# Routed experts moved into the block of the second graph layer, with gathers two blocks ahead

## The reference

```python
x = x + gnn(layernorm(x))      # two layers: aggregate over edges, add the residual product, relu
y = layernorm(x)
logits = softmax(relu(y @ router_w1 + b1) @ router_w2 + b2)
top_w, top_i = top_k(logits, 2); weights = softmax(top_w)
h1 = relu(y @ expert_w1[e] + b1[e]); h2 = relu(h1 @ expert_w2[e] + b2[e])
x = x + sum over the two chosen e of weight * (h2 @ expert_w3[e] + b3[e])
```

## Time and profile before

| | us |
|---|---|
| median of 3 runs (2244.78 to 2249.43) | 2246.9 |
| the profiled execution | 2250.68 |
| its span | 2249.0 |
| busy PE, DVE, ACT, POOL | 1913.3, 1201.6, 828.8, 334.9 |

### The profile page before, as it was taken

The page is one execution under the profiler, slowest core; times in us unless marked ns, Lnnn a source line. Parts: engine busy times, 40 slices in busy tenths (PEclk is TensorE's granted clock), DMA queues, the critical chain, the costliest instruction groups (busy, mean ns, idle before and its releaser), DMA issues. The chain is left out here.

```text
span 2249.0 us, 38317 instructions
## 1 busy us (share of the span) xinstructions
PE 1913.3 (85%) x12396; PEld 1155.2 (51%) x12396; DVE 1201.6 (53%) x2678; ACT 828.8 (37%) x1921; POOL 334.9 (15%) x350
## 2 busy tenths in 40 slices
PE   3458917999999999999979999999997199986765
PEld 3444504555555555555535555455554088865554
DVE  8995606666666666666514444444444244433333
ACT  3805715565656556565502222221222022221111
POOL 1006100000000000000001111211212023344444
PEclk9999968999999999999989999999998599999999
DMA  6002283333223332333375454554553588855552
GB/s 197 0 0 63 68 162 88 143 141 138 109 111 142 138 138 97 125 142 138 132 293 189 171 213 182 182 217 167 200 198 111 174 267 269 276 171 203 190 198 93
DMA packets 117038, 350.59 MB, mean 156 GB/s; under 512 B 18798, under 2 KB 79942, under 8 KB 110712
## 3 DMA queue, kind: packets, MB, share of 16 engines
q1 hardware_dynamic: 90140, 297.18, 37.6%
q0 software_dynamic: 16480, 40.14, 5.3%
q10 hardware_dynamic: 10364, 12.64, 1.7%
HBM read 209.41 MB, written 150.46 MB: 160 GB/s over the span
## 5 line engine op out<-in xcount | busy, mean ns | idle before, releaser
L1178 PE MATMUL bank<-parts,counts 128*128 128x512 f16 x2401 | 643.3, 378 | 0.0
L1178 PE MATMUL bank<-parts,counts_again 128*128 128x512 f16 x2401 | 540.2, 380 | 11.8 <-DMA counts_again<-counts_table 10.5
L1325 ACT ACTIVATE counts<-bank 128x392 f16<-128x392 f32 x800 | 395.1, 497 | 363.4 <-PE bank L1241 356.7
L1178 PEld LDWEIGHTS bank<-parts,counts_again 128*128 128x128 f16 x2401 | 235.5, 100 | 280.4 <-issue 14.1
L580 DVE TENSOR_TENSOR rows_lo<-pair_keys,iota_lo 128x2048 bf16<-128x2048 bf16 x200 | 245.0, 1225 | 239.2 <-PE bank L1241 239.2
L1241 PEld LDWEIGHTS bank<-rows_hi,rows_lo 128*128 128x128 bf16 x3200 | 227.6, 99 | 256.8 <-DVE rows_hi L580 65.3
L1241 PE MATMUL bank<-rows_hi,rows_lo 128*128 128x98 bf16 x3200 | 277.9, 210 | 64.0 <-DVE rows_hi L580 63.1
L454 POOL DMA_INDIRECT first_rows<-route_rows,route_spot_i x49 | 48.2, 984 | 1402.0 <-DVE tokens L445 1394.7
L1178 PEld LDWEIGHTS bank<-parts,counts 128*128 128x128 f16 x2401 | 192.5, 96 | 103.6 <-issue 1.1
L580 DVE TENSOR_TENSOR rows_hi<-pair_keys,iota_hi 128x1568 bf16<-128x1568 bf16 x200 | 193.8, 969 | 0.0
L1949 ACT ACTIVATE h_t<-bank,w 128x256 f32<-128x256 f32 x120 | 56.9, 474 | 295.1 <-PE bank L1898 295.1
(11 more groups left out here) (223 smaller groups left out, 1981.8 us busy)
## 6 DMA issues: line engine op xcount, KB each, us to landing
counts_table<-counts SPq DMA_DIRECT2D x25, 3136.0 KB, 9.2
counts_again<-counts_table SPq DMA_DIRECT2D x24, 3136.0 KB, 12.8
w<-expert_pack SPq DMA_DIRECT2D x60, 898.0 KB, 5.2
rows<-first_rows SPq DMA_DIRECT2D x30, 514.0 KB, 6.7
res_tile<-res_table SPq DMA_DIRECT2D x98, 128.0 KB, 2.2
rows<-second_rows SPq DMA_DIRECT2D x30, 258.0 KB, 5.0
res_table<-res_tile SPq DMA_DIRECT2D x49, 128.0 KB, 1.7
res_table<-res_next SPq DMA_DIRECT2D x49, 128.0 KB, 6.2
```

What stands on the lines that cost most here:

```text
L1178: mm = nc.tensor.matmul(acc[:, 0:2 * dim], lhs, rhs, start=s == 0, stop=s == tiles)
L1325: nc.scalar.activation(counts[:, b, :, :].rearrange("p s (o n) -> p o s n", o=2)[:, :, :, q * QUAD:(q + 1) * QUAD], bank[4 + q % 4][:, 0:Q ...
```

## The change

The experts no longer have a block of their own. Their instructions stand in `sum_and_route`, behind or between those of the last pairs, in a class `Work` whose methods are called from each engine's code.

- VectorE makes an early list (`early_list`) while pair 23 is summed, from the rows placed up to pair 21. It holds 17 blocks of first choices (`EARLY_BLOCKS`) which are certain to be full. The rest of the list is made later (`final_list`).
- Blocks 0 to 5 are loaded as soon as the scatters of pairs 0 to 21 have landed and SP is through with its own last pair; the weights once pair 23 is summed, since they now lie in the second buffer of `counts_again`.
- The last part of routing is split over the steps of the first blocks by functions `beside(b)`, which each engine calls in its step b. The zeros behind each expert's rows are written by POOL in steps 8 to 13.
- `index` and `gather` are two blocks ahead instead of one, and `index(b + 2)` stands ahead of `add_bias(b)`. `outs` has one bank per block and signals once per block, and waits for the result of two blocks ago instead of one.
- `turn` has one bank in place of two, and the router's four banks are now one. The marks for `count_before` are bf16.

```diff
@@ sum_and_route, SP
                     by_pairs(sp, pair)
+                    work.early_rows(sp)
+                    sp.wait_ge(update.sums_ready, 2 * LAST_PAIR)
+                    work.early_weights(sp)
+                    work.loads(sp)
@@ TensorE
+                    def beside(b):
+                        if b == 0:
+                            pe.wait_ge(update.sums_out, tiles)
+                        if b == 1:
+                            router.count_before(pe, LAST_PAIR - 1, 2)
+                        if b == 4:
+                            router.turn(pe, LAST_PAIR, 0, 1)
+                        if b == 5:
+                            router.hide(pe, LAST_PAIR, 1)
+                        if b == 6:
+                            router.logits(pe, LAST_PAIR, 1)
+                        if b == 8:
+                            router.count_before(pe, LAST_PAIR, 1)
+                    work.products(pe, beside)
@@ VectorE
+                    def beside(b):
+                        if b == 0:
+                            router.choices(dve, LAST_PAIR - 1, 2, False)
+                        if b == 1:
+                            router.gates(dve, LAST_PAIR - 1, 1, 2)
+                        if b == 2:
+                            router.place(dve, LAST_PAIR - 1, 1, 2, False)
+                            router.variance(dve, LAST_PAIR, 1)
+                        if b == 3:
+                            router.normal_rows(dve, LAST_PAIR, 0, 1)
+                        if b == 6:
+                            router.shift_logits(dve, LAST_PAIR, 1)
+                        if b == 7:
+                            router.choices(dve, LAST_PAIR, 1, True)
+                        if b == 8:
+                            router.gates(dve, LAST_PAIR, 0, 1)
+                            router.place(dve, LAST_PAIR, 0, 1, True)
+                            work.free_rows(dve)
+                        if b == 9:
+                            work.final_list(dve)
@@ class Work
+                def loads(self, sp):
+                    def after(first):
+                        def body(b, k):
+                            sp.wait_ge(result_ready, b + 1)
+                            self.load_weights(sp, b + WB, k)
+                            if first is not None:
+                                self.load_rows(sp, b + SB, k, first)
+                        return body
+                    for b in range(2 * SB):
+                        if b + SB == EARLY_BLOCKS:
+                            sp.wait_ge(list_ready, 2)
+                            sp.wait_ge(rest_cleared[0], 16 * experts)
+                            router.wait_scattered(sp, pairs)
+                        after(True)(b, b)
...
+                def add_outs(self, dve, b, k, c):
+                    dve.wait_ge(bias_added, b + 1)
+                    dve.wait_ge(outs_ready, b + 1)
...
+                    def steps(r, c, start=False, last=False):
+                        for k in range(SB):
+                            b = r * SB + k
+                            self.high(dve, b, k, 1, h2_bank, h2_t, h2_ready, h2_high_out)
+                            if not (last and k + 1 >= SB):
+                                self.high(dve, b + 1, (k + 1) % SB, 0, h1_bank, h1_t, h1_ready, h1_high_out)
+                            if isinstance(b, int) and b < 2 * SB:
+                                beside(b)
+                            if not (last and k + 2 >= SB):
+                                into = 1 if isinstance(r, int) and b + 2 >= NB else c
+                                self.index(dve, b + 2, (k + 2) % SB, r + (k + 2) // SB, into)
+                            if c:
+                                dve.wait_ge(first_back[k % 3], (r - NB // SB) * (32 * SB // 3) + 32 * (k // 3 + 1))
+                            self.add_bias(dve, b, k, c)
...
+                            self.add_outs(dve, b, k, c)
...
+                    for b in range(3 * SB):
+                        self.scatter(pool, b, b, first_out)
+                        beside(b)
+                        if b == 8:
+                            pool.wait_ge(free_ready, 1)
+                        if 8 <= b < 8 + len(clears) // 2:
+                            for c, e in clears[2 * (b - 8):2 * (b - 7)]:
+                                self.clear(pool, c, e)
...
+                    for b in range(NB, NB + 2):
+                        self.gather(pool, b, b)
+                    def second(b, k):
+                        self.gather(pool, b + 2, k + 2)
+                        self.scatter(pool, b, k, out)
```

More of the change, by code:

```diff
@@ L236, with __init__ @@
     STEPS = 36
-    def __init__(self, nc, sb, sem, shapes, tables, weights, consts, placed_to, tokens, banks):
+    def __init__(self, nc, sb, sem, shapes, tables, weights, consts, placed_to, tokens, turns):
         self.nc = nc
@@ L455, in scatter, with wait_scattered_to @@
                                         bounds_check=table.shape[0] - 1, oob_is_err=False).then_inc(self.scattered[b], 16)
+    def wait_scattered_to(self, eng, i):
+        for b in range(2):
+            eng.wait_ge(self.scattered[b], SCATTERS * 16 * ((i + 1) // 2))
     def wait_scattered(self, eng, pairs):
@@ L474, in gnn_moe_kernel @@
     K2 = dim // P
+    pairs = -(-tiles // 2)
     ROWS = 2 * P
@@ L480, in gnn_moe_kernel @@
     table_rows = experts * region + idle * ROWS
+    EARLY = pairs - 4
+    EARLY_BLOCKS = -(-((EARLY + 1) * 2 * P - experts * (ROWS - 1)) // ROWS)
     W_COLS = 3 * K2 * dim + 2 * K2 + dim
-    pairs = -(-tiles // 2)
     slots = 64
@@ L1472, in pair @@
                         p, pj, pb = before_pair(i, j, b)
-                        stops = (units,) if first else ROUTE_AT + (units,)
+                        stops = [units]
+                        if not first:
+                            stops += [at for at in ROUTE_AT if at < units]
+                        if last:
+                            stops += EXPERTS_AT
                         done = 0
-                        for k, to in enumerate(stops):
-                            to = min(to, units)
+                        for to in sorted(stops):
                             sum_units(pe, counts, b, i, done, to, update.sums_out, update.sums_ready, first, chunk_back if first else None)
@@ L1533, in _, with beside @@
                     by_pairs(pool, pair)
-                    router.scatter(pool, pairs - 1, 0, 1)
-                    router.wait_scattered(pool, pairs)
+                    def beside(b):
+                        if b == 2:
+                            router.scatter(pool, LAST_PAIR - 1, 1, 2)
+                        if b == 8:
+                            router.scatter(pool, LAST_PAIR, 0, 1)
+                    work.moves(pool, beside)
                 @block.vector
@@ L1557, in pair @@
                         p, pj, pb = before_pair(i, j, b)
-                        sums(p, pj, pb, 1, is_first(p))
-                        route(p, pb, 2, False)
+                        sums(p, pj, pb, 1, is_at(p, 0))
+                        router.variance(dve, p, 2)
+                        router.normal_rows(dve, p, pb, 2)
+                        if is_at(p, EARLY + 1):
+                            work.early_list(dve)
+                        if last:
+                            work.first_high(dve)
+                        router.shift_logits(dve, p, 2)
+                        if last:
+                            sums(i, j, b, 0, False)
+                            return
+                        router.choices(dve, p, 2, False)
                         sums(i, j, b, 0, False)
@@ L1609, in _ @@
                     router.make_ranks(dve)
+                    work.begin_list(dve)
                     by_pairs(dve, pair)
+                    work.early_list(dve)
+                    work.free_rows(dve)
+                    work.final_list(dve)
+                    work.first_high(dve)
+                    work.high_halves(dve, nothing)
                 @block.scalar
@@ L1622, in _ @@
                     by_pairs(act, pair)
+                    work.first_copies(act)
+                    work.first_low(act)
+                    work.low_halves(act, nothing)
                 @block.tensor
@@ L1633, in _ @@
                     by_pairs(pe, pair)
+                    work.first_turns(pe)
+                    work.first_hidden_layer(pe)
+                    work.products(pe, nothing)
                 @block.gpsimd
```

720 lines of the change are left out of this document (375 added, 345 removed).

## The result

The changed kernel took 2135.7 us (median of 4 runs, 2130.3 to 2137.8) where the kernel before took 2248.2 beside it: a ratio of 0.9496, 95% interval 0.9473 to 0.952. 2139 had been predicted. The profiled execution took 2134.5 us with a span of 2133.0, that of before 2249.0.

What follows compares the result with a forecast made beforehand. TensorE was taken to bound pass 1, and a chain of wait, bias, index, issue and landing pass 2. Terms summed to -108.3 us, from 2249.0 to a span of 2140.7, so 2139; range for 8 in 10: 2107 to 2170.

Steps and rivals of the forecast that it cites:

- The start: Between the last sums and block 0: its result starts at 1740.7 instead of 1805.36, -64.7 us.
- the wait for the first weights: At the start of the experts: TensorE waits perhaps 1.2 us, since six row loads stand ahead of the weights.
- Routing beside pass 1: Pass 1: +15 us lag from VectorE's routing, +2 TensorE's routing matmuls, +4 zeros, +3 late signal of `outs`.
- the late signal of `outs`: Pass 1: `outs` signals once, so results start later by between nothing and 0.2 us a step; 0.1 taken, +3 us.
- the zeros: Pass 1, steps 8 to 13: POOL's zeros compete with weights for bytes, nothing to 8 us, +4 taken.
- The loop of the weights: Result, weights request, landing, first layer three blocks later: no slack at 5.62 us a step, so late results delay TensorE.
- Pass 2: Gathers issued two blocks ahead: waits for them all but vanish, pace 8.39 to 6.1 us a block, -61.8 us.
- the loop has slack: Rival, chance 0.16: weights land sooner, pace 5.75 us in both passes and half the lag absorbed, 2111 us.
- POOL isn't held up: Rival, chance 0.19: VectorE's evictions hold POOL's four issues in pass 2, 7.2 us a step, 2169 us.
- slower than before: Rival, chance 0.03: POOL's zeros hold scatters and VectorE in six steps, at 12 us each 2262 us.
- The seam: Between the passes: block 30 again 13.7 us after block 29, blocks 29 to 32 take 25.3 us, not 31.1, -5.8.
- The end: From the last result to the end of the kernel: stays 11.5 us, no change.

Runs made afterwards that it cites:

- c1: Changed kernel with first weights asked for after two row loads, block 14's before the wait for zeros, later weights released by products and bias, list ends later: 2125.0 us.
- s2: Changed kernel with SP's first loads reordered, the first weights asked for after the rows of blocks 0 and 1: 2200.5 us, ratio 0.9569, on another chip.
- c2: c1 with rows of blocks 17 to 19 held back until weights of 14 to 16 are asked for, then the wait for list and zeros: 2122.8 us.
- a1: The changed kernel itself, run once more on another chip beside s5, z2 and c2: 2142.1 us, ratio 0.9514.
- g1: Changed kernel with gathers issued one block ahead again, the index still two blocks ahead and before the wait for the gather: 2153.9 us, ratio 0.9562.
- s5: Changed kernel with weights of block b+3 released by the products and bias of block b, not its result: 2129.8 us, ratio 0.9456.
- g3: Changed kernel with both cuts undone, gathers one block ahead and the index of block b+1 behind the bias: 2216.1 us, ratio 0.9845.
- s1: Changed kernel with block 14's weights asked for at block 11 before SP waits for list, marks' scatters and zeros: 2203.8 us, ratio 0.9586, another chip.
- s4: Changed kernel with the last six instructions of the list in step 10 instead of step 9: 2202.6 us, ratio 0.9589, on another chip.
- z2: Changed kernel with ten more loads of zeros added to the twelve, SP waiting for all: 2158.1 us, ratio 0.9583.

## Why the prediction was right

**The start, 64.7 us (3 of them given back in block 0).** Taken from the last load of `x_tile`, the start went from 1805.36 - 1715.40 = 90.0 us to 31.7, by 58.2 where 61.7 were expected. The term was 3.5 us too large, and the experiment says which part: the wait for the first weights, put at 1.2 us, was 3.67 us, with a slow first layer behind it (1.5 us more), and c1, s2 and c2, which ask for the weights earlier, have 5.3 us less. I had priced the bytes of the six row loads at the 269 GB/s of pass 1 (11.7 us) and had no row for how long weights asked for behind them take to land. SP's first row load is at 1720.00 and its request for the first weights, behind all six, at 1727.85; they land 8.0 us later, with the DMA engines busy throughout (share 0.99 from 1720 to 1736). TensorE was ready at 1732.2. In c2 the request comes 2.7 us after the first row load and takes 8.2 us to land, so it is the place in the order that counts. The other 3.2 us of the 55.0 lie ahead of the change: the loads of the last pair began at 1718.6 instead of 1715.4, and the changed code was at 1713.8 in a1. That is the scatter of this kernel.

**Routing beside pass 1, +15 +2 +4 +3 and 3 of it in block 0.** Measured 13.0 us more than before from result 0 to 29 in the profiled execution. The three executions with the changed kernel's code for this part (this one, a1 and g1) took 187.4, 194.1 and 195.4 us, so on the mean 17.9 more than before, against 21; of before there is one. The sum of the term was fair; its parts were not. The 3 us of choices in block 0 are there (8.9 us from its second layer to its result, 5.7 before). From block 0 to 8 the results lose 52.1 - 8 x 5.62 = 7.1 us, where 4 were put (7 less those 3), and the list loses another 5.2 in step 9. The 0.1 us a step for the late signal of `outs` was wrong: blocks 17 to 29 are 5.62 us apart. And the zeros, put at 4 between bounds of 0 and 8, were too cheap. At 5.62 us a step blocks 9 to 17 would take 45 us, before they took 47.8; they took 57.1 and in a1 62.2, with the zeros under way in them. I had priced bytes that compete, and this is what the changed kernel's own hole at block 12 is, only dearer: one weight load took 10.7 us. Left out was that SP waits for the last of the zeros with a weight load queued behind, which made the hole in a1. What made up for it: the forecast counts from a pass 1 that lost 11.4 us itself (174.4 against 163.0 at 5.62), 3.3 of them in blocks 17 to 29. Of these the profiled execution loses none, a1 1.5 and g1 2.8.

**The loop of the weights.** I took it for the cause of the pace in both passes, 6.1 us. It exists: released 0.8 to 1.0 us earlier it gives back 12 us (s5 against a1, 10 of them in pass 2 and at the seam). But its size was off. I took the landing of the earlier trace rows, 5.7 us, plus 2.07 from result to request, and found no slack. But the 2.07 of the earlier trace rows are block 0's alone: over pass 1 of the kernel before, the median is 1.70, so that 7.4 us stood in 7.8. This is the term that was mis-sized. After the change the request again comes 1.7 us after the start of the result, an undisturbed first layer of block b+3 starts 7.5 us after it, and the landing is 5.0 in the even part of pass 1: 6.7 us in 7.5, slack, and a pace of 5.62. In pass 2 the landing is 5.6 (6.3 in a1), the loop is about closed (not held in a1: 8.0 in 7.5), and the pace is 5.80 (5.99). Two rows of pass 2 in the changed kernel show the request:

```profile
2034.97 0.88 DVE L2060 SCALAR_TENSOR_TENSOR both_w<-bank,rows,both_w 128x256 f32<-128x256 f32 x2
...
2036.66 0.33 SPq L1831 DMA_DIRECT2D counts_again<-expert_pack  x1
```

**Pass 2, -61.8.** Measured -70.0; the mechanism is g3's: undo both cuts and 8.54 us a step come back. The size is the pace, 5.80 instead of 6.1, for the reason above. The rival "the loop has slack" (5.75, 2111 in all) was right in this term, and wrong in expecting half the lag of pass 1 to be absorbed. I had not seen that one cut would do: the distance alone is enough, and the index ahead of the wait gives more than four fifths (6.22 us a step, between 8.54 and 5.80).

**The other rivals.** POOL isn't held up. Its issues in pass 2 (x count, busy us, mean ns, idle time before):

```profile
L2120 POOL DMA_INDIRECT out_dram<-both_w,to_token x54 | 55.5, 1028 | 18.0 <-issue 15.2 <-DVE both_w L2060 1.8 <-DVE to_token L2071 0.9
L2113 POOL DMA_INDIRECT rows<-first_out,to_token x51 | 52.8, 1035 | 29.0 <-issue 15.9 <-DVE to_token L2071 7.8 <-DVE both_w L2060 5.2
```

They take 1.03 us with VectorE busy for half of the stretch, and took as much before, when it was busy for a third; 7.2 us a step would have needed 1.5. The prediction spoke of the evictions, which read PSUM; `add_bias` (L2052) reads tensors in SBUF only, and the issues beside it were hardly longer: the longest of pass 2 took 1.23 us. The Trainium skill ("SBUF — State Buffer", section "SBUF: two separate sides") says that VectorE can keep GpSimd from writing the descriptors of its DMAs, with fp32 copies from SBUF to SBUF as the case. No issue here grew so, but VectorE makes no such copies in pass 2, so these runs don't test it. A zero load takes POOL 0.78 us, far from the 10.7 at which "slower than before" decided.

**The seam**, -5.8, was -6.2, with block 30 at 13.5 us after block 29. **The end**, taken as unchanged, is 2.3 us longer: the last scatter is issued 1.75 us after the result as before, and the rest of the time lies behind it, 9.8 us after the end of the last issue instead of 7.5. All later kernels have it (13.0 to 14.3 us). Why is open.

**How near the sum came.** The span was 2133.0 us, 7.6 below the forecast 2140.7. That is the balance of larger errors: the start gave 6.7 us less than expected and the end 2.3, pass 1 cost 8.0 less, and pass 2 and the seam gave 8.6 more. In a1, the same code, the five terms are 59.7, -19.8, 5.9, 64.8 and -2.3, together the forecast 108.3. So the mechanisms of the start, the seam and pass 2 were right, and how near the total came is in part luck.

Open too is the chip on which s1 to s4 ran. The last load of `x_tile` begins 40 to 55 us later there, pass 2 takes 6.5 us a step, and the traces put part of the waits down to events that they don't show.

## What to carry to other kernels

When a stage is bound by a chain that closes on itself (wait, bias, index, issue, landing), look for any one link that doesn't need its predecessor; a second cut adds little. Follow every loop of a prefetch in numbers (request, landing, use) for each stage by itself, since the landing differs with the load: a request that hangs on the last reader, rather than on the result, is a small edit and was worth 12 us. Take such times from many steps: one request read from one block (2.07 us, where the median is 1.70) made a loop look closed that had slack. And of a queue in order, ask what stands behind each of its waits and issues: the first weights stood behind six loads of rows and need not have (5.3 us of the start). The weights behind SP's wait for the zeros need not have stood there either, but taking the last of them out (c2 against c1) gained nothing that the runs can tell, and there they landed late beside the zeros.

## What I had not expected of the hardware

TensorE's matmuls after a gap are often twice as slow, but the length of the gap doesn't say whether. After waits of 3.67, 3.30 and 4.33 us eight matmuls took 3.41, 3.75 and 3.78 us instead of 1.89, nearly all at the lower of the clock's two levels (1.2 instead of 2.4 GHz): the granted clock is 0.50 from 1815 to 1818 and from 1832 to 1835. After 2.38 us in c2 they took 3.58 (0.50 from 1830 to 1833), and after 3.26 us, one step before it, 1.99 (1.00 from 1821 to 1823). The eight behind them can be slow too: 3.16 us after the 3.75, 3.13 after the 3.78, but 2.03 after the 3.58. So such gaps cost from nothing to about 3 us beyond themselves.

A load of zeros of 514 KB from POOL takes 0.76 to 0.81 us to issue, but 10.0 us to land (median of the six), 12.6 in z2. The weights beside such loads took twice as long to land as otherwise (11.0 us in c2, 4.9 in an even stretch of the changed kernel).
